# Query features as squares of sums, made on TensorE, and a quotient taken token by token

## The reference

```python
def second_taylor_expansion(x):            # 1 + 16 + 256 features
    x2 = jnp.einsum('...i,...j->...ij', x, x) * 0.5 ** 0.5
    return jnp.concatenate([x0, x, x2.reshape(...)], axis=-1)
q = (normed @ w_q); k, v = normed @ w_kv;  q = q * dh ** (-0.5)
q, k = second_taylor_expansion(q), second_taylor_expansion(k)
kv_state = jnp.einsum('bhnd,bhne->bhde', k, v)
den = jnp.einsum('bhnd,bhd->bhn', q, jnp.sum(k, axis=2))
out = jnp.einsum('bhnd,bhde->bhne', q, kv_state) / jnp.maximum(den, EPS)
x = layernorm(x + out @ w_out)
h = silu(x @ w1.T * s1) * (x @ w2.T * s2)      # 128 -> 512
h = gelu(h @ h1.T * t1); h = gelu(h @ h2.T * t2)   # 512 -> 512, twice
x = layernorm(x + h @ w3.T * s3)               # 512 -> 128
```

## Time and profile before

| what | us |
|---|---|
| median of three runs | 689.7 |
| profiled execution | 689.84 |
| its span | 688.0 |
| TensorE matmuls busy | 632.4 (92%) |
| VectorE busy | 544.8 (79%) |
| ScalarE busy | 451.6 (66%) |
| GpSimd busy | 280.5 (41%) |
| transposes of query features on TensorE (640) | 97.6 |
| products of q on GpSimd (32) | 79.1 |
| reciprocals on VectorE (32) | 55.8 |

### The profile page before, as it was taken

How to read it: one execution, slowest core, us unless ns; L and a number is a source line. 1 busy time by engine, 2 the same in 40 slices (tenths; PEclk the granted TensorE clock), 3 DMA queues, 4 the chain that set the end, 5 groups by cost and what they waited for, 6 DMA issues and landing times.

```text
span 688.0 us, 13058 instructions
## 1 busy us (share of the span) xinstructions
PE 632.4 (92%) x4385; PEld 455.9 (66%) x4385; DVE 544.8 (79%) x1017; ACT 451.6 (66%) x1002; POOL 280.5 (41%) x281
## 2 busy tenths in 40 slices
PE   3473999999999999999999999999999999999985
PEld 2342767676776868676776767676776767676663
DVE  2676587978889797978979797988979797886763
ACT  3562558676675858677585867677585867666563
POOL 4955233343454344254454434344443434341000
PEclk9886999999999999999999999999999999999998
DMA  6000000000100000010000001010000001000000
GB/s 220 1 0 17 2 3 13 2 31 2 31 0 30 0 0 30 0 30 0 30 0 22 9 0 30 0 30 0 30 0 1 29 0 31 16 1 17 0 16 15
DMA packets 7224, 11.97 MB, mean 17 GB/s; under 512 B 800, under 2 KB 1824, under 8 KB 7200
## 3 DMA queue, kind: packets, MB, share of 16 engines
q1 hardware_dynamic: 7200, 11.65, 5.2%
HBM read 7.45 MB, written 4.19 MB: 17 GB/s over the span
## 4 chain that ended last, share of the span: by engine, by line
PE 56%; DVE 19%; issue 17%; POOL 4%; ACT 3%; DVEq 1%; DMA 0%; SPq 0%; POOLq 0%; ACTq 0%
PE fps L381 15%; PE fps L382 13%; PE acc L350 9%; PE ring L340 8%; PE ring L313 6%; DVE wide L727 4%; DVE hid_lo L804 3%; DVE phi_k L239 3%; PE acc L359 2%; DVE hid_lo L796 2%; DVE h L786 2%; PE ring L299 2%; DVE wide L725 2%; ACT gate_zo L595 2%; DVE wide L732 1%
## 5 line engine op out<-in xcount | busy, mean ns | idle before, releaser
L381 PE MATMUL fps<-hid_hi,w_hi 128*128 128x512 f32 x576 | 241.4, 419 | 10.2 <-DVE hid_lo L804 5.8
L382 PE MATMUL fps<-hid_lo,w_hi 128*128 128x512 f32 x576 | 227.5, 395 | 0.0
L604 ACT ACTIVATE hid_hi<-fps,col 128x512 fp32r<-128x512 f32 x128 | 88.4, 690 | 86.9 <-PE fps L382 86.9
L381 PEld LDWEIGHTS fps<-hid_hi,w_hi 128*128 128x128 f32 x576 | 108.2, 188 | 41.8 <-DVE hid_lo L804 13.2
L546 ACT ACTIVATE phiT<-ring 128x512 f32<-128x512 f32 x160 | 94.2, 602 | 44.7 <-PE ring L340 42.7
L382 PEld LDWEIGHTS fps<-hid_lo,w_hi 128*128 128x128 f32 x576 | 108.6, 189 | 16.2
L239 DVE TENSOR_TENSOR phi_k<-phi_k 128x1024 f32<-128x1024 f32 x64 | 104.5, 1637 | 8.6 <-ACT v_one L546 8.6
L340 PEld LDWEIGHTS ring<-const,phi_q 128*128 128x128 f32 x640 | 78.9, 144 | 39.3 <-issue 20.0
L340 PE MATMUL ring<-const,phi_q 128*128 128x128 f32 x640 | 97.6, 281 | 6.9 <-POOL phi_q L927 6.1
L804 DVE TENSOR_TENSOR hid_lo<-fps,hid_hi 128x512 fp32r<-128x512 f32 x128 | 84.6, 671 | 17.9 <-ACT fps L605 17.8
L927 POOL TENSOR_TENSOR phi_k<-phi_k 128x64 f32<-128x64 f32 x64 | 29.2, 456 | 164.6 <-ACT v_one L546 164.5
(11 more groups left out here) (83 smaller groups left out, 967.8 us busy)
## 6 DMA issues: line engine op xcount, KB each, us to landing
x_b<-in_x SPq DMA_DIRECT2D x16, 256.0 KB, 2.8
out<-gate_zo SPq DMA_DIRECT2D x16, 256.0 KB, 2.9
h<-in_h SPq DMA_DIRECT2D x1, 1024.0 KB, 8.6
gate_zo<-in_h SPq DMA_DIRECT2D x1, 1024.0 KB, 10.7
wide<-in_w SPq DMA_DIRECT2D x3, 256.0 KB, 4.0
w_qkv_raw<-in_w_kv SPq DMA_DIRECT2D x1, 128.0 KB, 2.6
const<-in_consts SPq DMA_DIRECT2D x1, 98.5 KB, 2.5
w_qkv_raw<-in_w_q SPq DMA_DIRECT2D x1, 64.0 KB, 2.5
```

The costliest lines, as they stand in the source:

```text
L381: nc.tensor.matmul(fps[:, bank, :], w_hi[:, o:o + P], hi, start=start, stop=False)
L382: mm = nc.tensor.matmul(fps[:, bank, :], w_hi[:, o:o + P], lo, start=False, stop=stop and not with_lo)
L604: nc.scalar.activation(hid[1 - layer][0][:, m, :], fps[:, bank, :], ACT.Gelu, scale=scale)
```

## The change

The projection now gives, for each token tile, only k, v and one more column for each head (half the sum of k's channels), 264 columns instead of 384; q is projected directly in transposed form, once for all tokens (three products of 512 columns). ScalarE copies q^T to a high part, in halves of 64 partitions, and to the linear rows of the rest features; VectorE writes the low part beside it on the other 64 partitions. A 0/1 selection matrix, a new input of 384 KB, is multiplied with these: eight products give sums q_i + q_j (and 2-fold entries), which ScalarE squares straight into the transposed features; a ninth pair gives the rest, squared with a bias of one. All forty transposes and copies of query features go, and so do VectorE's and GpSimd's products of q.

The weights that apply to these features follow from the state by its transposes; the main ones have numerator and denominator in one set, so eight main products replace sixteen. The rest weights are spread by GpSimd (`spread_rest`, three operations) into a 128x256 tile and transposed by TensorE (`transpose_rest`, a new entry right behind the transposes of x). ScalarE copies numerator and denominator to SBUF (`copy_numden`), TensorE transposes them (two groups of four), VectorE divides token by token (`normalise`) and TensorE transposes the attention back (four). GpSimd's order is now: spread, power for the tail, three operations on k for the first two tiles, power for x1, three for the other two, next x. VectorE's is: gate with x's low part in it, the sum for the tail, first product of k, both quotients, tail scaling, then GELU tiles with the second product of k, the low part of q^T, the sum for x1, and the other products of k between. k's products have 896 elements instead of 1024.

TensorE's new order in a step, feed-forward products (L1 to L4) in short: state; L1 tile 0; state transposes; L1 tile 1; x transposes, rest transposes; L1 tile 2; main application; L1 tile 3; rest application; y transposes; first k/v projection; L2 (tile 0: two); first quotient transposes; L2 one; second quotient transposes; L2 two; second projection; L2 one; attention transposes; L2 two; q^T; L2 two; output; L2 two; third projection; L2 four; fourth projection; L3 three; then nine sums, each with one to three L3 or L4 products between, and the x1 transposes before the last.

ScalarE: table load, state copy, gates, copies of x's high part and rest weights between the gates, quotient copies, first k/v copy, table load, second k/v copy, first GELU tile, attention copy, second GELU tile, the four copies of q^T, third GELU tile, third k/v copy, fourth GELU tile, fourth k/v copy, squares 0 and 1, two GELU tiles, squares 2 and 3, one, squares 4 and 5, one, squares 6 and 7, x1's high part, the ninth (two halves), y, square of the next x.

```diff
 RING = [(what, stage, n % 2) for n, (what, stage) in enumerate((
-    ("state", MIDDLE), ("stateT", MIDDLE), ("xT", FRONT),
-    ("phi0", MIDDLE), ("phi2", MIDDLE), ("qkv0", FRONT), ("phi4", MIDDLE), ("phi6", MIDDLE), ("qkv1", FRONT),
-    ("phi1", MIDDLE), ("phi3", MIDDLE), ("phi5", MIDDLE), ("phi7", MIDDLE), ("qkv2", FRONT), ("qkv3", FRONT),
-    ("out", MIDDLE), ("phi8", FRONT), ("phi9", FRONT)))]
+    ("state", MIDDLE), ("stateT", MIDDLE), ("xT", FRONT), ("restT", MIDDLE), ("kv0", FRONT), ("nt0", MIDDLE),
+    ("nt1", MIDDLE), ("kv1", FRONT), ("attT", MIDDLE), ("qT", FRONT), ("out", MIDDLE), ("kv2", FRONT), ("kv3", FRONT),
+    ("sq0", FRONT), ("sq1", FRONT), ("sq2", FRONT), ("sq3", FRONT), ("sq4", FRONT), ("sq5", FRONT), ("sq6", FRONT),
+    ("sq7", FRONT), ("sq8", FRONT)))]
 FPS = [(what, stage, n % 4) for n, (what, stage) in enumerate((
     ("a0", FFN), ("b0", FFN), ("a1", FFN), ("b1", FFN), ("a2", FFN), ("b2", FFN), ("a3", FFN), ("b3", FFN),
...
+            def project_q(t):
+                bank_wait(RING, ring_free, t, "qT")
+                for n, (x_part, w_part) in enumerate(((xnT_hi, w_qkv_hi), (xnT_hi, w_qkv_lo), (xnT_lo, w_qkv_hi))):
+                    mm = nc.tensor.matmul(ring[:, bank_of(RING, "qT"), :], w_part[:, KV:], x_part[:, :],
+                                          start=(n == 0), stop=(n == 2))
+                mm.then_inc(ring_full, 1)
+            def sums_of_q(t, f):
+                what = f"sq{f}"
+                if f == 0:
+                    pe.wait_ge(ring_free[bank_of(RING, "qT")], read(RING, t, "qT"))
+                bank_wait(RING, ring_free, t, what)
+                bank = bank_of(RING, what)
+                if f < H:
+                    mm = nc.tensor.matmul(ring[:, bank, :], sel[:, (f % 4) * P:(f % 4 + 1) * P], qT[f // 4][:, :],
+                                          start=True, stop=True)
+                else:
+                    nc.tensor.matmul(ring[:, bank, :], sel[:, 4 * P:5 * P], qT[0][:, :], start=True, stop=False)
+                    mm = nc.tensor.matmul(ring[:, bank, :], sel[:, 5 * P:6 * P], qT[1][:, :], start=False, stop=True)
...
+            def transpose_rest(t):
+                pe.wait_ge(st_rest_ready, t)
+                bank_wait(RING, ring_free, t, "restT")
+                for g in range(2):
+                    mm = nc.tensor.transpose(ring[:, bank_of(RING, "restT"), g * P:(g + 1) * P],
+                                             st_rest[:, g * P:(g + 1) * P], ident)
...
+            def apply_main(t):
+                pe.wait_ge(ring_free[bank_of(RING, "stateT")], read(RING, t, "stateT"))
+                for h in range(H):
+                    g, hh = h // 4, h % 4
+                    nc.tensor.matmul(acc[32 * hh:32 * hh + 32, g, :], w_main[:, 32 * h:32 * h + 32], phiT[:, h, :],
+                                     start=True, stop=False)
+            def apply_rest(t):
+                pe.wait_ge(ring_free[bank_of(RING, "restT")], read(RING, t, "restT"))
+                for g in range(2):
+                    for hh in range(4):
+                        h = 4 * g + hh
+                        mm = nc.tensor.matmul(acc[32 * hh:32 * hh + 32, g, :], w_rest[:, 32 * h:32 * h + 32],
+                                              restq[g][:, :], start=False, stop=True)
+                    mm.then_inc(acc_full, 1)
...
+            def copy_q(t):
+                act.wait_ge(ring_full, written(RING, t, "qT"))
+                bank = ring[:, bank_of(RING, "qT"), :]
+                nc.scalar.activation(qT[0][0:64, :], bank[0:64, :], ACT.Copy)
+                nc.scalar.activation(qT[1][64:P, :], bank[64:P, :], ACT.Copy)
+                nc.scalar.activation(restq[0][0:64, :], bank[0:64, :], ACT.Copy)
+                nc.scalar.activation(restq[1][64:P, :], bank[64:P, :], ACT.Copy).then_inc(q_hi_ready, 1)
+            def square_sums(t, *tiles):
                 for f in tiles:
-                    ring_copy(t, f"phi{f}", phiT[:, f, :], ring[:, bank_of(RING, f"phi{f}"), :])
+                    act.wait_ge(ring_full, written(RING, t, f"sq{f}"))
+                    bank = bank_of(RING, f"sq{f}")
+                    if f < H:
+                        op = nc.scalar.activation(phiT[:, f, :], ring[:, bank, :], ACT.Square)
+                    else:
+                        nc.scalar.activation(restq[0][64:P, :], ring[64:P, bank, :], ACT.Square, bias=one_c[64:P, :])
+                        op = nc.scalar.activation(restq[1][0:64, :], ring[0:64, bank, :], ACT.Square,
+                                                  bias=one_c[0:64, :])
+                    op.then_inc(ring_free[bank], 1)
...
+            def x_lo(t):
+                bank = bank_of(RING, "xT")
+                dve.wait_ge(x_hi_ready, t + 1)
+                nc.vector.tensor_tensor(xnT_lo[:, :], ring[:, bank, :], xnT_hi[:, :].bitcast(F32), ALU.subtract)\
+                    .then_inc(ring_free[bank], 1)
+            def q_lo(t):
+                bank = bank_of(RING, "qT")
+                dve.wait_ge(q_hi_ready, t + 1)
+                nc.vector.tensor_tensor(qT[0][64:P, :], ring[0:64, bank, :], qT[0][0:64, :].bitcast(F32), ALU.subtract)
+                nc.vector.tensor_tensor(qT[1][0:64, :], ring[64:P, bank, :], qT[1][64:P, :].bitcast(F32),
+                                        ALU.subtract).then_inc(ring_free[bank], 1)
+            def normalise(t, g):
+                bank = bank_of(RING, f"nt{g}")
+                nt = ring[:, bank, :].rearrange("p (j h e) -> p j h e", j=NT, h=4)
+                dve.wait_ge(ring_full, written(RING, t, f"nt{g}"))
+                nc.vector.tensor_scalar(den[:, g, :, :], nt[:, :, :, DEN], DEN_EPS, None, ALU.max)\
+                    .then_inc(den_ready, 1)
+                dve.wait_ge(den_ready, 2 * (t - 1) + g + 1)
+                nc.vector.reciprocal(rden[:, g, :, :], den[:, g, :, :]).then_inc(rden_ready, 1)
+                dve.wait_ge(rden_ready, 2 * (t - 1) + g + 1)
+                out = att_tok.rearrange("p (j h e) -> p j h e", j=NT, h=H)[:, :, 4 * g:4 * g + 4, :]
+                nc.vector.tensor_tensor(out, nt[:, :, :, 0:DH],
+                                        rden[:, g, :, :].unsqueeze(3).to_broadcast([P, NT, 4, DH]), ALU.mult)\
...
+            def spread_rest(t):
+                pool.wait_ge(ring_free[bank_of(RING, "state")], read(RING, t, "state"))
+                part, whole = st_rest[:, :].ap[0], st_rest[:, :]
+                lin = bass.AP(whole.tensor, whole.offset, [part, [P + 64, 2], [DH, 4], [1, DH]])
+                prod8 = bass.AP(whole.tensor, whole.offset + 64, [part, [64, 2], [8, 4], [1, 8]])
+                one = bass.AP(whole.tensor, whole.offset + 96, [part, [64, 2], [1, 1]])
+                nc.gpsimd.tensor_tensor(lin, st[:, :, LIN:FEAT].unsqueeze(2).to_broadcast([P, 2, 4, DH]),
+                                        mask_lin.unsqueeze(1).to_broadcast([P, 2, 4, DH]), ALU.mult)
+                nc.gpsimd.tensor_tensor(prod8, st[:, :, PROD8:ONE].unsqueeze(2).to_broadcast([P, 2, 4, 8]),
+                                        mask8.unsqueeze(1).to_broadcast([P, 2, 4, 8]), ALU.mult)
+                nc.gpsimd.tensor_copy(one, st[:, :, ONE:LIN]).then_inc(st_rest_ready, 1)
...
```

More of the change, by code:

```diff
@@ L563, in copy_state_T, with x_hi @@
-            def copy_state_T(t):
-                src = ring[:, bank_of(RING, "stateT"), 0:2 * P].rearrange("p (c b n e) -> p c b n e", c=4, b=2, n=2)
-                for nd in range(2):
-                    ring_copy(t, "stateT", w_main[:, nd, :, 0:4:3, :], src[:, :, :, nd, :], half_c, last=(nd == 1))
-            def copy_phi_T(t, *tiles):
-                for f in tiles:
-                    ring_copy(t, f"phi{f}", phiT[:, f, :], ring[:, bank_of(RING, f"phi{f}"), :])
+            def x_hi(t):
+                act.wait_ge(ring_full, written(RING, t, "xT"))
+                nc.scalar.activation(xnT_hi[:, :], ring[:, bank_of(RING, "xT"), :], ACT.Copy).then_inc(x_hi_ready, 1)
@@ L859, in step @@
                 if middle:
-                    normalise(t)
-                if front and not is_step(t, 0):
+                    sum_x1(t, 1 - par)
+                if front:
                     phi_k_main(t, 2)
@@ L864, in step @@
                     gelu_tile(t, 0, 3)
-                if middle:
-                    sum_x1(t, 1 - par)
                 if is_step(t, 1):
                     largest_lo()
-                if front and not is_step(t, 0):
+                if front:
                     phi_k_main(t, 3)
+                if middle:
+                    norm_scale(t - 1, x1p, mv, rstd, mv_ready, rstd_ready, x1[1 - par], x1_ready)
                 if ffn:
@@ L1006 @@
     row = _np.arange(128)
-    used = (row % 32 < DUP) | (row % 32 >= ONE)
-    head = (row[:, None] // 32 == _np.arange(4)[None, :]) & used[:, None]
+    head = row[:, None] // 32 == _np.arange(4)[None, :]
     data["consts"] = _np.concatenate([
```

(11 more changed lines are left out.)

435 lines of the change are left out of this document (209 added, 226 removed).

## The result

The changed kernel took 719.4 us (718.85 to 720.73, four runs) beside 689.4 us for the kernel before in the same job: ratio 1.043, 95% interval 1.041 to 1.044. I had forecast 704 us, at most 716. The direction was right, the size was half of what came.

What follows compares the result with a forecast made beforehand. TensorE was taken to bound the kernel. Its 36.1 us a step plus waits of 1.6, 0.7, 1.5 and 0.3 gave 40.2, so 688.0 + 16 - 3 + 2 = 703, with 1.84 outside the span 705, stated as 704 (681 to 716).

Steps and rivals of the forecast that it cites:

- the term for the start: First steps: x's low part behind VectorE's weight splitting, q^T's chain and nine sums, less two GpSimd products; +2 us (-3 to +6).
- The four waits: TensorE's waits in a full step: step start 1.6 us, quotient 0.7, copies of q^T 1.5, sums 0.3.
- TensorE's sum: TensorE's own work in a full step without waits: 6.9 us removed, 4.5 added, leaving 36.1 us.
- Late 1: Step start: state copy and GpSimd's spread of the rest weights come late for TensorE; 1.6 us lost (1.2 to 2.3).
- Late 2: Before the second k/v projection: VectorE's first quotient, behind k's first products, comes late; 0.7 us lost (0.2 to 1.5).
- Late 3: Before the third k/v projection: ScalarE's four q^T copies and VectorE's subtractions hold its bank; 1.5 us lost (1.0 to 2.0).
- Late 4: Sums near the step's end: the fifth waits for ScalarE's square of the third; 0.3 us lost (0 to 0.8).
- The step without a front: That one step saves about 4 us of TensorE's work, with 1 us of waits: -3 us.
- The rule on the clock: Whether new idle gaps throttle TensorE: clock expected to stay at 2.4 GHz; rival some 9 us longer steps, about 820, chance 0.03.

Runs made afterwards that it cites:

- The order of the copies alone: Changed kernel with ScalarE's four copies of q^T reordered, both of the lower half, then both of the upper half, nothing else: 713.6 us, ratio 1.034.
- The experiment on step 1: Changed kernel; in step 1 GpSimd spreads rest weights before its weight split, ScalarE's low-weight sums follow the attention and q^T copies: 714.7 us, ratio 1.035.
- The run with all edits: Changed kernel with quotients first, q^T copied by halves and projected earlier, next x squared earlier, rest transposes later: 667.4 us, ratio 0.967.

## Why the prediction was wrong

**In short.** The forecast was at 704 us (681 to 716), and 719.4 came. The step of the prediction that failed is the term for the start: I put +2 us for it, -3 to +6, and it was +10.95, because the spread of the rest weights and the attention copy, on which TensorE now depends in step 1, stand behind the weights' preparation on GpSimd and ScalarE. A second term was mis-sized, the copies of q^T in each full step. The four waits that I named in a full step came where I had them.

**TensorE's sum was right, and a little better.** I had 36.1 us without waits. The waits of the step above, with the restart of TensorE after each (the distance to the product before, less the usual 0.23), are 0.72 for the state copy, 0.18 for x, 0.70 for the rest weights, 1.2 for the quotient, 2.15 for q^T and 0.47 for the sums: 5.4 us. 40.87 - 5.4 = 35.5. The 264-column products are 0.12 apart (342.16 and 342.28), as priced. Most of the 0.6 that I had too much lies in the step before and not in a price: I took its waits as about 0.6 us in all, but two places alone cost 1.0 with their restarts. From 275.86, a group of four transposes, to the next product are 0.77 us for the usual 0.36:

```profile
276.63 0.50 PE L381 MATMUL fps<-hid_hi,w_hi 128*128 128x512 f32 x1 [0.16 <-DVE hid_lo L796]
```

and ahead of 297.00 it is 0.74 for 0.23, with 0.1 more at that product. So the sum before was 38.0 at most, and 38.0 - 2.4 is 35.6.

**Late 1, the start of the step: right.** I expected 1.6 us at the state copy and the spread, and 0.72 + 0.18 + 0.70 = 1.6 came. The square of x began 1.49 us after zero (I had 1.45). In the repeated step the spread is faster than I put it, 1.03 us for 1.25:

```profile
329.49 0.45 POOL L1020 TENSOR_TENSOR st_rest<-st,const 128x128 f32<-128x128 f32 x1
329.89 0.50 POOL L1022 TENSOR_TENSOR st_rest<-st,const 128x64 f32<-128x64 f32 x1
330.34 0.18 POOL L1024 COPY st_rest<-st 128x2 f32<-128x2 f32 x1
```

**Late 2, the quotient: 1.2 us for 0.7, within its bounds.** VectorE's product of k began 15.76 after zero (I had 15.6), and the quotient's three operations are 0.17, 0.25 and 0.43 long, 0.92 in all for my 0.88:

```profile
340.97 0.17 DVE L797 TENSOR_SCALAR den<-ring 128x16 f32<-128x16 f32 x1
341.17 0.25 DVE L800 RECIPROCAL rden<-den 128x16 f32<-128x16 f32 x1
341.46 0.43 DVE L803 TENSOR_TENSOR wide<-ring,rden 128x256 f32<-128x256 f32 x1
```

Here the size of VectorE's part was right; TensorE was there earlier than I had it (340.85, 16.65 after zero; I had 16.9), and it needs 0.15 to 0.2 to start again, which I hadn't counted.

**Late 3, the copies of q^T: 2.15 us for 1.5, above its bound of 2.0, the term of the full step that was mis-sized.** I had the first copy at K + 3.9 (K is the start of the second projection) and it began at 345.85 - 341.94 = 3.91; TensorE reached the third projection at K + 5.75 (I had 5.8). What lay between was mis-sized: three copy distances of 0.61, not 0.5, end the fourth at K + 6.32 for 6.0, and the two subtractions take 1.39 for 1.29, since the second starts 0.70 behind the first:

```profile
348.29 0.69 DVE L788 TENSOR_TENSOR qT<-ring,qT 64x512 fp32r<-64x512 f32 x1 [1.57 <-ACT restq L620]
348.99 0.69 DVE L789 TENSOR_TENSOR qT<-ring,qT 64x512 fp32r<-64x512 f32 x1
```

I had taken the distances from rows whose neighbours lie on the same partitions (0.48 to 0.60; the earlier trace rows). The order of the copies alone gives 0.23 us back, so that part is shown. The last 0.16 is TensorE's restart, which I hadn't counted.

**Late 4, the sums: 0.47 for 0.3**, a wait of 0.23 and the restart.

Together an undisturbed full step is 40.86 us where I had 40.2. Over the fourteen the growth is 1.60 us a step (573.4 - 551.0) for my 1.15, which is 6.3 us of the miss; with the 1.8 us of an undisturbed step it would be 25, but step 2 of the kernel before was itself long, 42.98 us.

**The start: +10.95 for +2, outside its range of -3 to +6, the largest miss and the step that failed.** I had a warning that turned out not to bind, that x's low part stands behind VectorE's split of weights, and priced mainly that. That low part was there at 44.15 us. The first projection of step 1 comes at 49.65 instead of 36.19, without a wait of its own, for another reason. TensorE's waits before step 2 (the first is step 0's chain of q^T):

```profile
20.21 0.59 PE L310 MATMUL ring<-w_qkv_hi,xnT_hi 128*128 128x264 f32 x1 [3.92 <-DVE qT L789]
...
43.53 0.69 PE L364 MATMUL ring<-const,st_rest 128*128 128x128 f32 x2 [7.42 <-POOL st_rest L1024]
...
60.41 2.05 PE L405 MATMUL ring<-w_o,att 128*128 128x128 f32 x8 [5.24 <-ACT att L597]
```

The second is GpSimd's, which has its weight split and then the spread:

```profile
34.12 3.45 POOL L239 TENSOR_TENSOR w_lo<-wide,w_hi 128x1536 fp32r<-128x1536 f32 x1
37.53 2.49 POOL L1020 TENSOR_TENSOR st_rest<-st,const 128x128 f32<-128x128 f32 x1
39.98 1.29 POOL L1022 TENSOR_TENSOR st_rest<-st,const 128x64 f32<-128x64 f32 x1
41.23 2.25 POOL L1024 COPY st_rest<-st 128x2 f32<-128x2 f32 x1
```

The three operations that take 1.03 us in a repeated step take 5.95 here. The earlier trace rows showed it before: 2502 ns was the longest of the old mask products. I used that row as the range of a price, and didn't ask in which step its longest stands. The third is ScalarE's three sums over the low weights, 5.7 us (54.00 to 59.68) in its order ahead of the attention copy; the old kernel had no copy there that TensorE waited for in this way. The experiment on step 1 moved both and gave 4.2 us back. The run with all edits leaves both in place and began step 2 at 73.25, also 4.2 sooner; both together made the start 8.6 us shorter (68.91, 2.4 behind the kernel before). So the two places are shown as 4.2 of the 10.95 us, and the orders in the repeated step, which act in step 1 too, as about as much. The 2.4 left over are near my +2, but I hadn't made that number from such terms, so that this is luck. One term among them I had named and not priced: at the end of step 1 the ten products with the selection matrix, with their waits for ScalarE and the transposes of x1 between them, take 67.47 to 74.87, 7.4 us, with the granted clock at 0.50 from 64 to 72 us; no run tests them alone.

**The step without a front: -4.0 for -3**, right.

**The rule on the clock.** I gave a fall of the clock 0.03, as a quarter of every step. In the kernel after a stretch at the lower of the two levels, 1.2 GHz, came in two of fourteen full steps, in two of my experiments in ten and in thirteen, and each cost about 1.55 us. So what the Trainium skill says (TensorE: Matmul & The Clock Gate, HAM oscillation), that idle gaps in a loop can throttle TensorE again in each round, happened here in a small form, behind an idle time of less than 2 us and not in every round. My statement that the clock stays at 2.4 GHz was wrong. It decided two experiments, not the result: in the kernel after it costs about 3 us.

**The size of the miss** is thus 9 us at the start and 6 in the full steps, of which the copies of q^T and the quotient are the main terms. My chances leaned the right way (0.70 for slower), but the upper end, 716, was too low even by my own bounds: the start's upper end (+6) and the full step's (40.9) together give 704 + 4 + 10 = 718.

## What to carry over

When a change relieves the bounding engine but puts new results between its instructions, its sum is only what can be had; the forecast is made by what arrives late, instruction by instruction, and the time lost is often only order. Here the same arithmetic took 719 us in one order and 654 in another, with the kernel before at 690. Each wait that is taken away must be followed to the next one in the same order, and the first steps, where the setup work of all engines lies between, need a sum of their own.

## What the runs showed of the hardware

- A neighbour on other partitions is not overlapped. ScalarE's copies on 64 partitions last 0.59 us wherever they stand and start 0.47 to 0.50 apart on the same half, 0.59 to 0.63 when the half changes (all steps of three runs); VectorE's subtractions 0.70 where others of their length follow at 0.60. The Trainium skill (VectorE: DVE Perf Modes, Two Vector instructions with no wait between them) has a model by which a Vector instruction that reads or writes from another start quadrant (a group of 32 partitions) than the one before starts only when the earlier ones have finished; the trace agrees (the first subtraction ends at 348.98, the second starts at 348.99). The Trainium skill (ScalarE: Activation LUTs, What ACT_TABLE_LOAD costs) gives an overlap of some 93 ns for neighbouring activations, which the 0.09 to 0.12 us here agree with on the same partitions, and not on changing ones.
- A copy of half the partitions costs as much as one of all of them: 0.59 us for 64x512 beside 0.60 for 128x512.
- Small GpSimd operations beside VectorE's long ones on SBUF last until these end: a copy of two elements per partition took 2.25 us, where it takes 0.18 otherwise. Each of the three ended just behind a VectorE instruction (its split of 5.48 us ended at 39.72, its cast at 41.11, its second split at 43.43; GpSimd's at 40.02, 41.27 and 43.48). VectorE is slowed too: that split of 128x2048 took 5.48 us beside GpSimd's split, and 2.29 in the run on step 1, where GpSimd's split came later and only its spread ran beside. The Trainium skill (GPSIMD Engine Reference, Key points) says that GpSimd shares its SBUF interfaces with VectorE and contends with VectorE's instructions that have two SBUF inputs; the trace agrees.
- The granted clock can fall to its lower level behind an idle time of TensorE of 1.9 us in a step in which it is busy for 90% of the time, for some 3 us, and didn't fall in a full step behind step 2 where the idle time was filled.
